# A convolution kernel on one core: the taps' transforms moved ahead of their output layer

## What is computed

```python
def rpe_coeffs(...):                       # position -> 256 taps
    t = coords @ rpe_in_w.T + rpe_in_b     # 2 -> 128
    for i in range(3):
        t = relu(simple_rms(t)) @ rpe_h_w[i].T + rpe_h_b[i]
    return relu(simple_rms(t)) @ rpe_out_w.T + rpe_out_b      # 128 -> 256

def tno2d(v, g):                           # circular convolution on 112 x 112
    vf = rfft2(v, s=(112, 112)); af = rfft2(placed(g))
    return irfft2(vf * af)[:, :, :56, :56, :]

u, v = silu(xn @ W_u.T + b_u), silu(xn @ W_v.T + b_v)
out = (u * tno2d(v, g)) @ W_o.T + b_o + shortcut
```

## Time and profile before

| | |
|---|---|
| median of 3 runs | 3543.01 us (3539.26 to 3554.57) |
| profiled execution | 3533.34 us, of it 3531.5 us span of instructions |
| TensorE busy | 3160.9 us (90%) |
| VectorE / ScalarE busy | 2083.4 / 1486.9 us |
| `make_taps` | about 318 to 588 us |
| `convolve` | about 588 to 2000 us |

### The profile page before, as it was taken

How to read it: one execution, slowest core, us unless ns; L and a number is a source line. 1 busy time by engine, 2 the same in 40 slices (tenths; PEclk the granted TensorE clock), 3 DMA queues, 4 the chain that set the end, 5 groups by cost and what they waited for, 6 DMA issues and landing times. The chain is left out here.

```text
span 3531.5 us, 106371 instructions
## 1 busy us (share of the span) xinstructions
PE 3160.9 (90%) x44223; PEld 2406.7 (68%) x44223; DVE 2083.4 (59%) x3840; ACT 1486.9 (42%) x3254; POOL 251.6 (7%) x162
## 2 busy tenths in 40 slices
PE   5686977999999999999999898589898989898887
PEld 4563324777777777777777544477777877777777
DVE  4453553666666666666666577455555555555553
ACT  3454422444444444444444344454444444444431
POOL 0000000000000000000000022211111111111111
PEclk8787978999999999999999999799999999999999
DMA  6886004111211211111112497655555555555552
GB/s 149 252 215 177 1 0 160 49 48 48 49 48 48 49 49 48 48 49 49 48 49 49 165 404 311 130 82 87 107 88 106 93 98 88 104 104 87 106 83 52
DMA packets 1033978, 351.36 MB, mean 99 GB/s; under 512 B 888569, under 2 KB 1005991, under 8 KB 1028519
## 3 DMA queue, kind: packets, MB, share of 16 engines
q1 hardware_dynamic: 710832, 198.81, 25.7%
q10 hardware_dynamic: 322807, 147.46, 15.3%
HBM read 174.01 MB, written 172.15 MB: 98 GB/s over the span
## 5 line engine op out<-in xcount | busy, mean ns | idle before, releaser
L751 ACT ACTIVATE x_half<-ps_x 56x228 f32<-56x228 f32 x1024 | 366.1, 357 | 671.8 <-PE ps_x L693 662.9
L801 DVE TENSOR_TENSOR terms<-spec,ps_z 112x456 f32<-112x456 f32 x1024 | 573.0, 621 | 33.8 <-PE ps_z L701 28.7
L708 PEld LDWEIGHTS ps_q<-inv_w,prod 112*114 112x114 f32 x4096 | 434.9, 180 | 27.5 <-issue 25.5
L708 PE MATMUL ps_q<-inv_w,prod 112*114 112x112 f32 x4096 | 451.0, 263 | 0.9 <-DVE prod L805 0.9
L701 PE MATMUL ps_z<-x_half,fwd_w 120*112 120x456 f32 x1024 | 446.4, 558 | 0.9
L811 DVE COPY y_sb<-ps_y 112x224 f32<-112x224 f32 x256 | 100.1, 391 | 414.2 <-PE ps_y L716 331.7
L1143 PE MATMUL ps_l<-q_mixed,k_blocks 32*64 32x64 f32 x12544 | 231.8, 220 | 74.1 <-issue 73.4
L1094 POOL TENSOR_TENSOR k_blocks<-k_mixed,same_of 128x896 f32<-128x896 f32 x112 | 193.8, 1730 | 1072.4 <-ACT k_mixed L1237 1072.4
L1143 PEld LDWEIGHTS ps_l<-q_mixed,k_blocks 32*64 32x64 f32 x12544 | 206.1, 133 | 88.5 <-issue 79.8
L1120 PEld LDWEIGHTS ps_s<-v_blocks 128*64 128x64 f32 x6272 | 200.9, 141 | 90.5 <-issue 79.2
L693 PEld LDWEIGHTS ps_x<-fwd_h,v_in 96*120 96x120 f32 x2048 | 256.2, 185 | 8.0 <-issue 3.2
(11 more groups left out here) (128 smaller groups left out, 4488.7 us busy)
## 6 DMA issues: line engine op xcount, KB each, us to landing
conv_in<-v_sb ACTq DMA_DIRECT2D x112, 256.0 KB, 3.3
v_in<-conv_in SPq DMA_DIRECT2D x256, 112.0 KB
qk_heads<-st_qk ACTq DMA_DIRECT2D x56, 476.0 KB, 4.7
qk_rows<-qk_heads SPq DMA_DIRECT2D x56, 476.0 KB, 6.7
conv_out<-y_sb ACTq DMA_DIRECT2D x512, 49.0 KB
y<-conv_out SPq DMA_DIRECT2D x8, 1792.0 KB, 13.5
x_in<-in_x SPq DMA_DIRECT2D x8, 1568.0 KB, 9.7
shortcut<-short ACTq DMA_DIRECT2D x8, 1568.0 KB, 6.3
```

Source lines behind the costliest of these rows:

```text
L708: last = pe.matmul(ps_q[0:2 * NF, c * NFFT:(c + 1) * NFFT], prod[b % 2][:, x, c * 2 * NF:(c + 1) * 2 * NF], k.inv_w[:, x, :], start=(x == ...
L751: last = act.activation(x_half[b % 2][to:to + SIDE, :, a], src, ACT.Copy)
L801: last = dve.tensor_tensor(terms[:, x, :], spec[a][:, s, :], ps_z[b % 2][z][0:NFFT, 0:PC], ALU.mult)
```

## The change

The two transforms of the taps (over p and over q) act on positions, and the output layer on features; so they can change places. After the change `make_taps` transforms the 128 features and puts the output layer on their spectra. The spectra of all 256 channels (`k.spec`, 2 x 256 x 57 numbers on 112 partitions) stay in SBUF; `t.G` is gone, and so are `taps`, `copy_taps` and `load_taps` in `convolve`.

For the transforms, positions have to lie on the partitions. So the last round works the other way about: the activations are the stationary operand, in pieces of 111 positions, and the weights move (16 matmuls of 128 columns to a step in place of 4 of 444); the bias takes 16 small matmuls in place of 4. The sum of squares is now along the columns, so ScalarE gets it with the square (`accum_out`), 16 squares of 128 columns to a step; four small matmuls (L505 of the changed kernel) turn the old norm. The reciprocal has 16 columns, and GpSimd multiplies by it (111 x 2048 to a step). `spread` and `normalize` are gone, and so is the wait at the start of a round. Then come 118 groups of matmuls, each into one of four PSUM banks, copied out by ScalarE and VectorE by turns: 32 groups of 4 matmuls (over p; stationary is one feature of `feat`, whose 111 numbers lie 512 bytes apart in SBUF), 29 groups of 4 matmuls of 224 columns (over q), 57 groups of 2 matmuls of 256 columns (the output layer, one for each frequency; its copies write numbers 228 bytes apart). The output bias is one matmul on frequency zero. One constant more is loaded at the start, and one row in `make_taps`.

```diff
@@ make_taps, TensorE
-                    if m == 0 and s == 0:
-                        pe.wait_ge(relu, i * W)
-                    pe.matmul(ps_t[j % 5][:, 0:RC], k.w[:, RH + r - 1, :], acts[:, at_cols(s * W + m)], start=True, stop=False)
+                    for x in range(4):
+                        at = (s * W + m) * RC + x * TAPS
+                        pe.matmul(ps_t[j % 5][0:TAPS, x * CH:(x + 1) * CH], acts[:, at:at + TAPS], k.w[:, RH + r - 1, :], start=(x == 0), stop=False)
...
+                for x in range(4):
+                    for m in range(W):
+                        row = slice(32 * m, 32 * m + 1)
+                        last = pe.matmul(ps_t[(i * W + m) % 5][0:TAPS, x * CH:(x + 1) * CH], norm[row, s, x * TAPS:(x + 1) * TAPS], hb[row, r - 1, :],
+                                         start=False, stop=(x == 3))
...
+                if s:
+                    pe.wait_ge(n_r, LAST + s)
+                for x in range(4):
+                    last = pe.matmul(ps_n[0:TAPS, x * 4:x * 4 + 4], norm[:, s, x * TAPS:(x + 1) * TAPS], k.ident[:, 0:128:32], start=True, stop=True)
...
-            for at in range(NRC):
-                pe.wait_ge(act_r, at + 1)
-                for h in range(2):
...
-                    pe.matmul(ps_t[2 * (at % 2) + h][:, 0:RC], k.w[:, RO + h, :], acts[:, at_cols(at)], start=True, stop=True).then_inc(g_ps, 1)
+            pe.wait_ge(act_r, STEPS)
+            pe.wait_ge(sqr, ROUNDS * NRC)
+            for e in range(EV):
+                if e >= 4:
+                    left(e - 4)
+                bank = banks[e % 4]
+                if e < T1:
+                    for x in range(4):
+                        last = pe.matmul(bank[0:TAPS, x * 2 * NF:(x + 1) * 2 * NF], feat[:, 0:TAPS, 4 * e + x], k.tap_p[:], start=True, stop=True)
+                elif e < T1 + T2:
...
+                    for f in range(f0, min(f0 + 2, NF)):
+                        for ri in range(2):
+                            last = pe.matmul(bank[:, (f - f0) * 2 * NFFT:(f - f0 + 1) * 2 * NFFT], half[:, ri * NF + f, :],
+                                             k.tap_q[:, 2 * ri:2 * ri + 2, :].rearrange("p a g -> p (a g)"), start=(ri == 0), stop=(ri == 1))
+                else:
...
+                        last = pe.matmul(to, fspec[:, f, ri * NFFT:(ri + 1) * NFFT], k.w[:, RO:RO + 2, :].rearrange("p a c -> p (a c)"), start=True, stop=not dc)
+                last.then_inc(e_ps, 1)
@@ make_taps, ScalarE and GpSimd
+                        for x in range(4):
+                            last = act.activation(junk[j % 2 * 4 + x][:], ps_t[j % 5][0:TAPS, x * CH:(x + 1) * CH], ACT.Square,
+                                                  accum_out=ss3[i % 2][:, m, x:x + 1])
...
+                pool.tensor_tensor(f, f, bcast(rinv[s % 2][:].rearrange("p m x -> p (m x)"), 2, CH), ALU.mult).then_inc(act_r, 1)
@@ convolve
-                    if b == 2 and inside(c + 1):
-                        sp.wait_ge(g_ps, c * 4 + 2)
-                        load_taps(c + 1)
...
-                    if b < 4 and inside(c + 1):
-                        taps(c + 1, b)
...
-                    if b < 4 and inside(c + 1):
-                        copy_taps(c + 1, a + 1, b)
...
-                    last = dve.tensor_tensor(terms[:, x, :], spec[a][:, s, :], ps_z[b % 2][z][0:NFFT, 0:PC], ALU.mult)
+                    last = dve.tensor_tensor(terms[:, x, :], k.spec[0:NFFT, s, bass.ds(c * CC, CC), :].rearrange("p c f -> p (c f)"),
+                                             ps_z[b % 2][z][0:NFFT, 0:PC], ALU.mult)
```

More of the change, by code:

```diff
@@ L419, in make_taps @@
+        fspec = big[:, 0:NF * 2 * NFFT].rearrange("p (f x) -> p f x", f=NF)
         rpe4 = sb("rpe_in4", [128, 128])
         hb = sb("rpe_h_b4", [128, ROUNDS - 1, 128])
+        ob = sb("rpe_out_b_row", [1, EXP])
         norm = sb("pos_norm", [128, STEPS, RC])
[L422 to L425, removed]
@@ L464, in linear @@
                     pe.wait_ge(relu, rectified(j - 5))
+            def linear(i, m):
+                r, s, j = i // STEPS, i % STEPS, i * W + m
+                bank_free(j)
                 if r == 0:
@@ L553, in _ @@
+            for i in range(ROUNDS * STEPS):
+                if 0 <= i - 2 < LAST:
+                    root(i - 2)
+                squares(i)
+                if i >= LAST:
+                    if i == LAST + 1:
+                        root(LAST)
+                    if i > LAST:
+                        root(i)
+            for e in range(0, EV, 2):
+                act.wait_ge(e_ps, e + 1)
+                leave(e, lambda to, src: act.activation(to, src, ACT.Copy)).then_inc(e_act, 1)
         @block.vector
@@ L599, in convolve @@
+            for i in range(ROUNDS * STEPS):
+                if 0 <= i - 2 < LAST:
+                    update(i - 2)
+                rectify(i)
+                if i > LAST:
+                    if i == LAST + 1:
+                        update(LAST)
+                    update(i)
+            for e in range(1, EV, 2):
+                dve.wait_ge(e_ps, e + 1)
+                leave(e, lambda to, src: dve.tensor_copy(to, src)).then_inc(e_dve, 1)
 def convolve(nc, t, k):
@@ L718, in back_h @@
                 last.then_inc(y_ps, 1)
-            for part in range(4):
-                taps(0, part)
             image_h(0, 0)
@@ L767, in store @@
                     act.dma_start(dst[x], y_sb[b % 2][x * SIDE:(x + 1) * SIDE]).then_inc(y_stored[b % 2], 16)
-            for part in range(4):
-                copy_taps(0, 0, part)
             act.wait_ge(cleared, 4)
@@ L1394, in build @@
         project_in(nc, t, k)
-        make_taps(nc, t, k)
-        convolve(nc, t, k)
+        with nc.sbuf_tensor("spec", [128, 2, EXP, NF], F32) as k.spec:
+            make_taps(nc, t, k)
+            convolve(nc, t, k)
         project_out(nc, t, k)
```

239 lines of the change are left out of this document (108 added, 131 removed).

## The result

| | before | after |
|---|---|---|
| median, first chip | 3543.91 us (4 runs) | 3453.28 us (4 runs, 3449.58 to 3473.01) |
| median, another chip | 3544.56 us (9 runs) | 3455.13 us (5 runs, 3451.88 to 3458.57) |
| profiled execution, first chip | 3533.34 us, span 3531.5 | 3453.9 us, span 3452.1 |
| first matmul of `make_taps` to first image transform | 272.9 us | 312.1 us |
| first to last `ps_y` group | 1375.5 us | 1258.1 us |

The changed kernel is faster: after over before 0.9752, interval 0.9731 to 0.9773 (the other chip: 0.9750, 0.9730 to 0.9771). The predicted 3463.5 us lies 10 us above the median, inside the range.

What follows compares the result with a forecast made beforehand. TensorE, busy 90% of the span, was taken to bound the kernel. Terms -118 - 7.4 - 34.9 + 80.8 = -79.5 on the median 3543.0 gave 3463.5 us; range 3450 to 3478, with rivals 3438 to 3498.

Steps and rivals of the forecast that it cites:

- last round with its tail: Last round of `make_taps` up to the transforms: 63.9 us in place of 98.8, so -34.9.
- `convolve`, -118: In `convolve`, 31 chunks lose their taps at 3.8 us each on TensorE's path; images then come every 4.93 us.
- Before the last round, -7.4: Earlier rounds of `make_taps`: two round-start waits go, -8.4; one more constant and row to load, +1.
- Step of the last round, 7.2: Last round of `make_taps`: squares, rectify, tile 3's `linear`, bias and hand-overs take 7.2 us a step, bounds 5.5 and 9.
- the clock falls in the gaps of the last round: Last round, one case of a dearer `make_taps`: half clock adds 2.3 us a step, +16; chance of that whole rival 0.15.
- Stall of the norm, +4.6: Last round, once: `n_ps` of step LAST + 1 waits for step LAST's update, holding up TensorE 4.6 us.
- Tail, 10.3: End of the last round: last squares, root, VectorE instructions and GpSimd's multiply with TensorE idle, 10.3 us.
- Over p, 45.8: Over-p transform: weight loads with a 512-byte step take 0.179 us each, 45.8 us in all.
- The first rival: Over-p transform: the stepped weight load costs nothing extra; 18.9 us less, 3445 us; chance 0.30.
- The +1.5 for the low clock behind GpSimd's multiply: Start of the transforms: TensorE's clock is down after GpSimd's multiply, costing 1.5 us.
- Copies covered: Transforms and output layer: copies out by ScalarE and VectorE, 1.07 us on VectorE, fit under 1.74 us for two groups.
- Start of `convolve`, 5.0: Ahead of the first image transform: memset, then the load of the first images landing some 3.5 us after issue, 5.0 us.

Runs made afterwards that it cites:

- experiment 4: Kernel before without the taps' matmuls and copies in `convolve`: with the `t.G` load kept 3425.48 us (ratio 0.9669), without it 3418.86 us (0.9657).
- experiment 6: Changed kernel with the four matmuls turning the old norm issued ahead of the next step's last tile: 3450.40 us, one time.
- experiment 1: Changed kernel with the over-p stationary operand read at steps of 1 to 128 numbers, four groups each: 3467.58 us, one time.
- experiment 2: Changed kernel with features stored feature by feature; VectorE's rectify reads PSUM with a step (first form) or writes with one (second): 3446.86 and 3449.30 us.
- experiment 3: Changed kernel with the copies of over p and the output layer writing side by side into other storage: 3465.59 us, one time.
- experiment 7: Changed kernel plus feature-by-feature storage, moved norm turn and divided last multiply (combination): 3433.22 us; without the moved turn 3439.86; changed kernel unedited (repetition) 3455.13.
- experiment 5: Changed kernel with the wait for the whole last round put back at the first step of rounds 1, 2 and 3: 3460.24 us, one time.

## Why the prediction was right

Each term against the profiled execution of the changed kernel:

| term | forecast | measured | difference |
|---|---|---|---|
| to the bias ahead of the last round | -7.4 | -7.2 | +0.2 |
| last round with its tail | 63.9 | 60.8 | -3.1 |
| transforms, output layer, load of the first images | 147.5 | 149.9 | +2.4 |
| fill of `convolve` (first `ps_x` to first `ps_y`) | unchanged | 15.4 for 12.9 | +2.5 |
| `convolve`, first to last `ps_y` | -118 | -117.4 | +0.6 |
| all behind it | unchanged | -2.6 | -2.6 |

They add up to 0.0, so the exact hit is luck: errors of 2 to 3 us that cancel. The 10 us between prediction and median are of another kind. The profiled run of before lay 9.7 us under the median of the first three, on which the forecast was put; the profiled run of the changed kernel lies 0.6 us above its own. Of the 9.7, some 4 are the start of `convolve` (experiment 4), where this execution of before had the higher clock. Executions spread by more than that, mostly in where the taps begin (331.8 to 344.4 us in the runs here) and in the attention.

- *`convolve`, -118:* right by its step. The last chunk of before was the right stretch to read: it held none of what the change takes away, and showed 4.93 us with everything else in place.
- *Before the last round, -7.4:* right in sum, not in parts. The second start gave 4.4 (9.7 before, 5.3 after), the first only 1.6 (10.2 before, 8.6 after): there TensorE had waited 2.58 us for the input round, and without the wait its next matmuls come at the lower clock (6 records of `linear` in 3.47 us from 362.43, where before they took 2.50 from 366.15), which takes 1.0 of it back. I had read both from the start of the last round. The loads brought 1 us back in place of costing 1; the place of the first matmul varies by more.
- *Step of the last round, 7.2:* measured 6.34 and 7.19 by turns. The squares were the mis-sized part: four in 1.0 us, not 1.3. `ACTIVATION_READ_ACCUMULATOR` stands behind each square and lasts 0.19 to 0.32 us, but the next square starts 0.10 us after it began, so a square with its sum comes every 0.25 us. The bias took 1.07 (forecast 1.4): the four row groups do run side by side. That each second step is 0.85 longer goes with the clock: those steps have it at 0.76, the others at 1.00. The rival "the clock falls in the gaps of the last round" did come, for 0.85 us in each second step and not 2.3 in each. In experiment 6 all take 6.8 at full clock, so there the step is longer and steadier; what sets 6.8 was not tried.
- *Stall of the norm, +4.6:* right in place and size (4.62), and experiment 6 confirms the cause.
- *Tail, 10.3:* measured 8.9, by the shorter squares and by GpSimd's 3.61 for 3.95.
- *Over p, 45.8:* the step "a write with a long step on VectorE is the nearest row for a load with a long step on TensorE" gave 0.179 a load, measured 0.190 (48.7 us). Right to 6%, but as a stand-in only: experiment 1 shows that the price goes by pieces of 16 bytes and is the same from 64 bytes on, and experiment 2 that ScalarE's square, the row for "costs nothing", was no guide. The first rival is out. Side by side a load takes 0.097, not the 0.105 put for it. The +1.5 for the low clock behind GpSimd's multiply did not come here: the slow loads take 0.19 at 1.2 and at 2.4 GHz alike, and what the clock cost fell on over q.
- *Over q, 43.3, and output layer, 49.9:* 44.8 and 49.8. The former started at the lower clock (below); without that it takes 43.0.
- *Copies covered:* right, experiment 3; 1.08 to 1.10 us each under 1.73.
- *Start of `convolve`, 5.0:* right. Not priced was the fill behind it, 15.4 us at a mean clock of 0.71 for 12.9 at 0.87 before. This +2.5 can't be put down to the change: with the kernel before's own start the fill took 15.3 us at 0.70 in both runs of experiment 4.

## What to carry to other kernels

Read the price of a stage without the work that is to go from a stretch of the trace that already lacks it (here the last chunk); that beats any sum over durations. Where an operand becomes a matmul's stationary one, lay it out so that the numbers of a load lie side by side: where loads were what limited the matmuls, this was worth 21.5 us of 48.7 (with every second number used a load would cost 6% more than side by side, with every fourth twice as much). Storing it the other way cost VectorE nothing, since the step went to the side that reads PSUM, and GpSimd's multiply 0.9 us, which shows in the tail. A wait off the bounding engine's path is worth nothing, even 90 us of it; and a stretch of several idle microseconds on TensorE can cost twice, once as a wait and once as the slower start behind it (in the changed kernel the first image transform, behind a wait of 5.0 us, took 1.95 us for 1.00 later). The same clock makes one profiled execution a weak base: look at a second one of the same code before a difference of 2 us is explained.

## What the runs showed of the hardware

- A weight load of 111 float32 numbers at a granted clock of 1.00: 0.097 us with the numbers side by side (experiment 2), 0.104 at a step of 8 bytes, 0.153 at 12, 0.20 at 16, 0.21 at 32, 0.19 at 64, 256 and 512 (experiment 1). At a granted clock of 0.50 it takes 0.19 side by side and 0.19 at 512 bytes.
- Slow loads and the clock. Over q begins after a 1.1 us wait in all these kernels but that of experiment 3 (0.8). Windows of TensorE at its start, in the changed kernel and in the combination of experiment 7 (length, busy, clock):

```profile
530.00:545.00 15.00, 14.42 (x76) 1.00 0.00 1
545.50:550.00 4.50, 4.48 (x15) 0.64 0.00 0
```

```profile
505.00:520.00 15.00, 15.00 (x156) 1.00 0.01 1
520.00:524.00 4.00, 2.90 (x17) 1.00 0.00 0
```

  Behind the slow loads the granted clock fell to 1.2 GHz (0.64 on average over the first 4.5 us here, 0.50 over 5.5 us in the repetition of experiment 7) although the engine had been busy all the time and waited for 1.1 us only; behind the fast loads it stayed at 2.4 GHz. From its first to its last record over q took 44.6 to 46.3 us in five of six executions with slow loads, 43.0 in the sixth, and 43.0 in all four with fast ones. So in five of six the slow loads went with 1.6 to 3.2 us more than their own time; why the sixth (experiment 5) kept the clock is open.
- GpSimd multiplies 111 x 2048 numbers by a broadcast factor in 3.61 us where they lie in one run and the factor is constant along 128 of them, and in 4.53 where they lie in runs of 16 and each of the 16 has its own factor. Which of the two differences costs the 0.92 us was not tried.
